# Selective scan, C rows: by DMA through DRAM instead of by matmul and copy; three PSUM pairs in turn

## The reference, cut to what matters

```python
def selective_scan(xs, dts, As, Bs, Cs, Ds, dt_bias):
    delta = jax.nn.softplus(dts + dt_bias[None, :, :, None])
    ...
    def step(h, inp):
        d_t, x_t, B_t, C_t = inp
        dA = jnp.exp(d_t[..., None] * As)
        h = dA * h + (d_t * x_t)[..., None] * B_t[:, :, None, :]
        y = jnp.einsum('bkdn,bkn->bkd', h, C_t)
        return (h, y)
    ...
    return ys + Ds[None, :, :, None] * xs
```

## Time and profile before

| | |
|---|---|
| runs, median (lowest to highest) | 884.73 us (884.34 to 886.65), 3 runs |
| the profiled execution's own time | 886.18 us |
| its span, first to last instruction | 884.3 us |
| mean granted TensorE clock | 0.919 |
| PE, DVE, ACT, POOL busy | 79, 72, 53, 48% of the span |

### The profile page before, as it was taken

How to read it: one execution, slowest core, us unless ns; L and a number is a source line. 1 busy time by engine, 2 the same in 40 slices (tenths; PEclk the granted TensorE clock), 3 DMA queues, 4 the chain that set the end, 5 groups by cost and what they waited for, 6 DMA issues and landing times. The chain is left out here.

```text
span 884.3 us, 7771 instructions
## 1 busy us (share of the span) xinstructions
PE 696.2 (79%) x2716; PEld 366.0 (41%) x2716; DVE 636.9 (72%) x603; ACT 465.5 (53%) x505; POOL 425.5 (48%) x231
## 2 busy tenths in 40 slices
PE   3778788988787878877877786566476769999998
PEld 2443232323222323322322222245324568888886
DVE  5286998998998989998999987945693253334332
ACT  3477578787694787776866734214102223233231
POOL 5035978989989889798797630000051000000000
PEclk9969998999998999999999998879596579999999
DMA  5000000000000000000000006020630000000000
GB/s 154 0 1 1 0 1 1 0 1 0 0 1 0 1 0 1 0 0 1 0 1 0 1 8 254 0 103 1 238 142 1 0 1 1 0 0 0 0 0 24
DMA packets 8287, 20.74 MB, mean 23 GB/s; under 512 B 1333, under 2 KB 2071, under 8 KB 7519
## 3 DMA queue, kind: packets, MB, share of 16 engines
q1 hardware_dynamic: 8256, 20.37, 6.4%
HBM read 19.76 MB, written 0.61 MB: 23 GB/s over the span
## 5 line engine op out<-in xcount | busy, mean ns | idle before, releaser
L552 POOL TENSOR_TENSOR area<-area 128x1024 f32<-128x1024 f32 x127 | 300.1, 2379 | 94.4 <-DVE area L1075 72.7
L1075 DVE TENSOR_TENSOR_SCAN area<-area,ps 128x1024 f32<-128x1024 f32 x128 | 292.6, 2286 | 11.6
L1364 PE MATMUL ps<-area,cst 128*128 128x512 f32 x512 | 263.9, 640 | 30.4 <-POOL area L552 30.2
L735 ACT ACTIVATE area<-ps 128x1024 f32<-128x1024 f32 x127 | 129.8, 1022 | 108.9 <-PE ps L1329 107.8
L1068 DVE TENSOR_TENSOR ps<-ps,area 128x1024 f32<-128x1024 f32 x128 | 154.8, 1210 | 25.9 <-PE ps L1329 25.9
L728 ACT ACTIVATE area<-area,floors,par_sb 128x1024 f32<-128x1024 f32 x128 | 157.4, 1231 | 3.1 <-DVE area L1086 3.0
L1364 PEld LDWEIGHTS ps<-area,cst 128*128 128x128 f32 x512 | 91.1, 196 | 143.9 <-issue 95.8
L1629 PE MATMUL ps<-stack 128*128 128x512 f32 (+3 forms) x768 | 127.8, 326 | 0.4 <-DVE stack L1255 0.4
L1329 PE MATMUL ps<-stack,sel 32*128 32x512 f32 x512 | 86.2, 501 | 48.1 <-DVE area L1075 27.0
L1629 PEld LDWEIGHTS ps<-stack 128*128 128x128 f32 x768 | 117.0, 192 | 11.9 <-issue 2.6
L1329 PEld LDWEIGHTS ps<-stack,sel 32*128 32x128 f32 x512 | 34.8, 186 | 161.9 <-DVE area L1075 61.9
(11 more groups left out here) (285 smaller groups left out, 684.9 us busy)
## 6 DMA issues: line engine op xcount, KB each, us to landing
area<-phi_scaled SPq DMA_DIRECT2D x1, 4104.0 KB, 24.0
area<-in_m_phi_dram SPq DMA_DIRECT2D x4, 1024.0 KB, 8.5
area<-phi_scaled SPq DMA_DIRECT2D x1, 4096.0 KB, 13.7
area<-in_q_t_dram SPq DMA_DIRECT2D x1, 1024.0 KB, 15.2
area<-in_dft_dram SPq DMA_DIRECT2D x1, 784.0 KB
area<-in_m_u_dram SPq DMA_DIRECT2D x1, 768.0 KB, 6.1
area<-in_conv_w_dram SPq DMA_DIRECT2D x1, 576.0 KB, 6.4
cst<-in_consts_dram SPq DMA_DIRECT2D x1, 516.5 KB, 7.0
```

The lines of the kernel that those rows point to most:

```text
L552: pool.tensor_tensor(scan_order(prod[:, u % PRODS, :], k), lines(state[:, u % STATES, :], k), lines(c_sb[:, u % COPIES, :], k), MUL).then_ ...
L735: act.activation(c_sb[:, u % COPIES, :], banks(4), ACT.Copy).then_inc(sig("c_copied"), 1)
L1075: dve.tensor_tensor_scan(state[:, u % STATES, :], decay[:, u % DECAYS, :], drive_pair(u), 0.0, MUL, ADD).then_inc(sig("scanned"), 1)
L1364: mm = pe.matmul(ps[:, 6 + h, :], con("center"), half(prod[:, u % PRODS, :], h), start=False, stop=(u % (UNITS // 2) == UNITS // 2 - 1), s ...
```

## The change

PE no longer spreads C and ACT no longer copies it. When ACT has rounded a block's rows, SP writes the 16 C rows of the two halves from SBUF to a DRAM tensor (two DMAs a block), and for each unit reads one row back, broadcast to 128 partitions, into one of the three C buffers, once the product that used the buffer is made. POOL waits for that DMA instead of the copy.

PSUM pairs 0, 2 and 4 now turn among B spreads and jobs, in the order of a list `slots`; the use of slot s waits until slot s-3 is free, which for a B spread is its scan and for a job ACT's copy. ACT serves a job three units before the unit that it is listed with. PE sums with a lag: at a slot that waited for scan v it sums up to unit v-2, at most two. POOL's preparing sums stand behind units 4, 6, 8 and 10 of a block, one after the other unit; some spectral steps move to later blocks. DVE's list is in the same order as before (drive, scan, unit by unit), with the last C taken from SBUF.

```diff
+        LAG = 2
...
+        c_dram = nc.dram_tensor("c_rows", [BLOCKS, NS, L], F32)
...
+        def c_landed(engine, u):
+            engine.wait_ge(sig(f"c_in_{u % COPIES}"), 16 * (u // COPIES + 1))
...
+        EXTRA = {1: ("spec", 0), 2: ("spec", 1), 3: ("skip", 0), 5: ("var", 0)}
+        JOB_BEFORE = {2: ("gate", 0)}
+        for _n in range(BLOCKS - 1):
+            JOB_BEFORE[NS * _n + 5] = ("z", _n + 1)
+            JOB_BEFORE[NS * _n + 9] = ("rows", _n + 1)
+            if _n in EXTRA:
+                JOB_BEFORE[NS * _n + 13] = EXTRA[_n]
+        slots = []
+        for _u in range(UNITS):
+            if _u in JOB_BEFORE:
+                slots.append(JOB_BEFORE[_u])
+            slots.append(("b", _u))
+        BANK = {turn: 2 * (at % 3) for at, turn in enumerate(slots)}
+        BANK["z", 0], BANK["rows", 0], BANK["gate", 1] = 4, 2, 6
+        FREED = {"z": "relu_ready", "b": "scanned", "rows": "rows_rounded", "gate": "z_ready", "spec": "spec_out",
+                 "skip": "skip_copied", "var": "var_logged"}
+        SERVED = {u - 3: turn for u, turn in JOB_BEFORE.items() if u > 2}
+        OUT_AT, VAR_AT = BANK["b", UNITS - 3], BANK["b", UNITS - 2]
...
         def drive_pair(u):
-            return banks((0, 2)[u % 2])
-
-        Z_AT, ROWS_AT = 1, 2
-        JOBS = {}
-        for _n in range(1, BLOCKS):
-            JOBS[8 * (_n - 1) + Z_AT] = ("z", _n)
-            JOBS[8 * (_n - 1) + ROWS_AT] = ("rows", _n)
-        JOBS[8 + 4], JOBS[8 + 6], JOBS[2 * 8 + 4], JOBS[4 * 8 + 4] = ("spec", 0), ("spec", 1), ("skip", 0), ("var", 0)
-
-        turns = [("z", 0), ("c", 0), ("c", 1)]
-        for _m in range(PAIRS):
-            if _m in JOBS:
-                turns.append(JOBS[_m])
-            turns += [("c", _u) for _u in (2 * _m + 2, 2 * _m + 3) if _u < UNITS]
-            if _m == 0:
...
+            def c_rows_out(n):
+
+                sp.wait_ge(sig("rows_rounded"), n + 1)
+                src = c_raw(n)
+                for h in range(2):
+                    at = 64 + 32 * h
+                    sp.dma_start(c_dram.ap()[n, :, h * HALF:(h + 1) * HALF],
+                                 src[at:at + NS, :]).then_inc(sig("c_rows_out"), 16)
+
+            c_rows_out(0)
+            for u in range(UNITS):
+                n, i = divmod(u, NS)
+                if i == 0:
+                    sp.wait_ge(sig("c_rows_out"), 32 * (n + 1))
+                wait(sp, sig("weighed"), u - COPIES + 1)
+                sp.dma_start(c_sb[:, u % COPIES, :],
+                             c_dram.ap()[n, i:i + 1, :].broadcast_to([P, L])).then_inc(sig(f"c_in_{u % COPIES}"), 16)
+                if i == 10 and n < BLOCKS - 1:
+                    c_rows_out(n + 1)
...
             def weigh(u):
 
                 pool.wait_ge(sig("scanned"), u + 1)
-                pool.wait_ge(sig("c_copied"), u + 1)
+                c_landed(pool, u)
...
+            for u in range(UNITS - 1):
+                n, i = divmod(u, NS)
+                weigh(u)
+                if n < BLOCKS - 1:
+                    if i in (4, 6, 8, 10):
+                        soft_sum(n + 1, (i - 4) // 2)
+                    elif i == 9:
+                        split_rows(n + 1)
...
                 act.wait_ge(sig("rows_done"), n + 1)
                 wait(act, sig("rows_ready"), n)
                 if n:
-                    act.activation(rows_raw, ps[:, 4, :], ACT.Copy)
-                act.activation(high(rows_high), ps[:, (4 if n else 2), :], ACT.Copy).then_inc(sig("rows_rounded"), 1)
+                    wait(act, sig("c_rows_out"), 32 * n)
+                src = ps[:, BANK["rows", n], :]
+                if n:
+                    act.activation(rows_raw, src, ACT.Copy)
+                else:
+                    act.activation(c_raw(0)[64:128], src[64:128], ACT.Copy)
+                act.activation(high(rows_high[0:64]), src[0:64], ACT.Copy).then_inc(sig("rows_rounded"), 1)
...
-            def copy_c(u):
-
-                act.wait_ge(sig("c_spread"), u + 1)
-                wait(act, sig("weighed"), u - COPIES + 1)
-                act.activation(c_sb[:, u % COPIES, :], banks(4), ACT.Copy).then_inc(sig("c_copied"), 1)
...
+            act.preload_act_table_set("silu_and_others")
+            conv_out(1)
+            gate_out(0)
+            gate_out(1)
+            act.preload_act_table_set("natural_log_exp_and_others")
+            act.wait_ge(sig("phi_out"), 16)
+            for u in range(UNITS):
+                n, i = divmod(u, NS)
+                if u + DECAYS < UNITS:
+                    make_decay(u + DECAYS)
+                if u in SERVED:
+                    serve(*SERVED[u])
+                if i == 3 and n < BLOCKS - 1:
                     soft(n + 1, "exp")
                     soft(n + 1, "one_plus")
-                elif p == ROWS_AT and n < BLOCKS - 1:
+                elif i == 4 and n < BLOCKS - 1:
                     soft(n + 1, "log")
                     soft(n + 1, "rest")
...
-            for m in range(PAIRS):
-                n, p = divmod(m, 8)
-                for u in (2 * m, 2 * m + 1):
-                    drive_unit(u)
-                    scan_unit(u)
+            for u in range(UNITS):
+                drive_unit(u)
+                scan_unit(u)
...
+            def slot_free(at):
+
+                kind, i = slots[at - 3]
+                pe.wait_ge(sig(FREED[kind]), i + 1)
 
             def spread_b(u):
+
                 n, b, k, i = block_of(u)
                 if i == 0:
                     pe.wait_ge(sig("rows_ready"), n + 1)
-                wait(pe, sig("scanned"), u - 1)
-                spread(u, 0, (0, 2)[u % 2]).then_inc(sig("b_spread"), 1)
-
-            def spread_c(u):
-                n, b, k, i = block_of(u)
-                if i == 0:
-                    pe.wait_ge(sig("rows_ready"), n + 1)
-                shared_free("c", u)
-                spread(u, 1, 4).then_inc(sig("c_spread"), 1)
+                for h in range(2):
+                    at = 32 * h
+                    mm = pe.matmul(ps[:, BANK["b", u] + h, :], sel[at:at + 32, i, :], b_rows[at:at + 32, n % 2, :],
+                                   start=True, stop=True)
+                mm.then_inc(sig("b_spread"), 1)
...
             pe.wait_ge(*after("sel_ready"))
             spread_b(0)
             spread_b(1)
-            spread_c(0)
             convolution(1, 1)
-            spread_c(1)
+            gate(0)
             pe.wait_ge(sig("consts_in"), 16)
-            for m in range(PAIRS):
-                before, beside = sums_of(m)
-                pe.wait_ge(sig("scanned"), 2 * m + 1)
-                if 2 * m + 2 < UNITS:
-                    spread_b(2 * m + 2)
-                if m in JOBS:
-                    job(*JOBS[m])
-                if m == PAIRS - 1:
-                    pe.wait_ge(sig("first_gated"), 1)
-                    for h in range(2):
-                        project_out(0, h, y_first)
-                for u in before:
-                    sum_state(u)
-                pe.wait_ge(sig("scanned"), 2 * m + 2)
-                if 2 * m + 3 < UNITS:
-                    spread_b(2 * m + 3)
-                if 2 * m + 2 < UNITS:
-                    spread_c(2 * m + 2)
-                for u in beside[:1]:
-                    sum_state(u)
-                if 2 * m + 3 < UNITS:
-                    spread_c(2 * m + 3)
-                for u in beside[1:]:
-                    sum_state(u)
-                if m == 0:
-                    gate(0)
+            scanned, done = -1, 0
+            for at in range(3, len(slots)):
+                kind, i = slots[at]
+                if (kind, i) == ("b", 4):
                     gate(1)
-            sum_state(UNITS - 1)
+                slot_free(at)
+                if kind == "b":
+                    spread_b(i)
+                else:
+                    job(kind, i)
+                if slots[at - 3][0] == "b":
+                    scanned = slots[at - 3][1]
+                if i >= 4 or kind != "b":
+                    for u in range(done, min(done + 2, scanned - LAG + 1)):
+                        sum_state(u)
+                        done = u + 1
+            pe.wait_ge(sig("scanned"), UNITS - 1)
+            pe.wait_ge(sig("first_gated"), 1)
+            for h in range(2):
+                project_out(0, h, y_first)
+            for u in range(done, UNITS):
+                sum_state(u)
```

More of the change, by code:

```diff
@@ L166, in program, with c_raw @@
         high = lambda t: t.bitcast(F32R)
+        def c_raw(n):
+            return rows_raw if n else y_first[:, 0:HALF]
         w_dt_sb = c_sb[0:RANK, 0, :].rearrange("p (a k m) -> p a k m", a=2, k=ND)
@@ L749, in _ @@
             rows_round(0)
-            make_decay(0)
-            make_decay(1)
-            copy_c(0)
-            make_decay(2)
-            make_decay(3)
-            copy_c(1)
+            for u in range(DECAYS):
+                make_decay(u)
             def gate_out(b):
```

(28 more changed lines are left out.)

141 lines of the change are left out of this document (42 added, 99 removed).

## The result

The kernel after takes 863.95 us median (863.09 to 865.1, 4 runs), the kernel before, measured beside it, 885.39 us (884.34 to 886.65, 4 runs): ratio 0.9758, 95% interval 0.9739 to 0.9777, faster. The forecast was 866, range 861 to 877. The profiled execution took 863.64 us, its span 861.9.

The account below looks back on a forecast made before the run. DVE was taken to bound the scan stage, with holes ended by spreads on PE. The terms -25.9 + 1.5 + 3.6 + 2.3 = -18.5 us gave 867.7 from the profiled 886.18, by the median 866; range 861 to 877.

Parts of the forecast that it names:

- What bounds: Scan stage: DVE bounds it, with holes that each end with a spread on PE; drives wait 25.9 us.
- -25.9 for the waits: Scan stage: all 25.9 us that DVE's drives wait for spreads on PE go.
- The third pair as the cause: PSUM in the scan stage: B spread waits for scan u-3 instead of u-2, 7.0 us before its drive.
- The start, +1.5: B spread of unit 5, behind z, skip product and sum: 1.5 us late, between 0 (full clock) and 5.1 (lower clock).
- C by DMA, 3.5 us, cost 0: Each unit's C row broadcast to 128 partitions in 3.5 us, within the 8.1 us before its weighing: cost 0.
- the ring: C buffers: weigh, load, weigh over three units, period (load + 2.38) / 3, if the load takes over 8.1 us.
- POOL's backlog: Units 4 to 10 of a block: POOL falls behind by up to 5.3 us, 9.3 allowed: cost 0.
- PE clock 1.00: Scan stage: PE idles 1.0 us in every 3.5 and keeps clock 1.00 through the stage.
- The end, +3.6 + 2.3 = +5.9: After the last scan: two more units of sums left, +3.6 us; some 4.6 us at half clock lose 2.3.
- A: Projections in the stage: PE loses the clock, 1.4 us late at eight of 18 jobs, 11 us, 877; chance 0.12.
- B: C load takes over 8.1 us; at 9 us the period is 3.79, +37, so 903; chance 0.08.
- C: ACT serves a projection late, the spread inheriting its pair waits; 15.7 of 25.9 us stay, 882; chance 0.06.

Follow-up runs that it names:

- run 3: Kernel after, but B spreads alternate between two PSUM pairs and all jobs have the third, C still by DMA: 864.27 us, ratio 0.976 to the kernel before.
- run 4: Kernel after, but C spread by PE and copied by ACT again, no DMA, three pairs turning among B, C and jobs: 917.5 us, ratio 1.0358 to before.
- run 7: Kernel after with two C buffers instead of three: 864.5 us, ratio 0.9747 to the kernel before; with one buffer: 1188 us, one run.
- run 5: Kernel after with two pairs for B, one for jobs, and sums up to unit 124 drained before the last projection: 863.93 us, ratio 0.9722 to before.
- Run 6: Kernel after with PE's sums one unit behind instead of two: 867.11 us, ratio 0.9767 to the kernel before.
- Run 2: Kernel after with the sums of units 123 and 124 placed before the wait for the last projection: 859.61 us, ratio 0.9702 to the kernel before.
- run 1: The kernel after measured once more, unchanged: 864.77 us, ratio 0.9771 to the kernel before.

## Why the prediction was right, step by step

- **What bounds.** Right. DVE's holes, all ended by B spreads, were the whole price, and the earlier trace rows had it in one number.
- **-25.9 for the waits.** Right in kind, 1.7 short. From the first drive to the end of the last scan 27.6 us went. Most of the rest is overlap. Two rows in order of time, after:

```profile
52.36 2.29 DVE L1088 TENSOR_TENSOR_SCAN area<-area,ps 128x1024 f32<-128x1024 f32 x1
...
54.57 1.21 DVE L1081 TENSOR_TENSOR ps<-ps,area 128x1024 f32<-128x1024 f32 x1
```

  An unhindered drive starts 0.08 us before the scan ahead has ended (54.65), while a wait is counted from the scan's end; and a drive after a wait takes 1.23 instead of 1.21 us. With 13 waits that is 1.3 us.
- **The third pair as the cause.** Half wrong. The prediction put the gain down to two things at once, C gone from PE and ACT and B spreads a unit earlier. Runs 3 and 4 part them: C by DMA with two pairs gives 0.976, three pairs without the DMA 1.0358 (in the one order that was tried). The earlier spread gave 0.9 us of slack at the change of image, and no time that the runs could tell.
- **The start, +1.5.** The mechanism was right and the size a toss: 0 in the first execution, 1.51 and 1.53 in two others with the same order there, by whether z gets the full clock after 1.42 us of idleness. The ends 0 and 5.1 were rightly kept.
- **C by DMA, 3.5 us, cost 0.** 3.7 measured, and POOL never waited for it in either execution of the kernel after. The clean price of the ring is in run 7. That 128 partitions read the same 4 KB did no harm: 512 KB took 3.7 us, the median of 128 loads in a row.
- **POOL's backlog.** At most 5.3 us was predicted. Scan 61, and the weighing of units 61 and 62, after:

```profile
258.89 2.29 DVE L1088 TENSOR_TENSOR_SCAN area<-area,ps 128x1024 f32<-128x1024 f32 x1
```

```profile
265.53 4.66 POOL L576 TENSOR_TENSOR area<-area 128x1024 f32<-128x1024 f32 x2
```

  265.53 less 261.18, the end of the scan, is 4.35 us, the largest before the end of the stage. In the first block it is 3.3 us: there the four preparing sums take 2.4 us each, not the 2.95 I charged; the mean of the third of them over the blocks is 2.9. Cost 0, as predicted.
- **PE clock 1.00.** Right in every stretch from 60 to 480 us. The reason given, short idleness, is not the whole of it: in run 5 the clock fell at 282 us behind a hole of 0.44 us. Run 6 shows how near the edge is.
- **The end, +3.6 + 2.3 = +5.9.** Measured +5.6: 3.9 for the sums and 1.7 for the clock, which only the projection paid. Run 2 takes both back.
- **Not foreseen.** The first drive at 44.0 instead of 45.5, and +1.1 behind the last sum. The sum on paper was -18.5, the execution gave -22.5: the start term that did not come (1.5), the first drive (1.5), the overlap (1.7), 0.3 at the end, less 1.1. By the medians the change gave 21.4 us where 18.5 were forecast. So 866 against 863.95 is a sum with the main term right and several small ones missed, nearly all to the same side, not precision.
- **Rivals.** A: in the kernel after PE lost its clock at no projection between the start and the end of the stage; it lost it at z of the start in run 1, and at the output projection, both of which the forecast had in its own terms. B: its ring is real, its threshold far off. C: no wait came back behind ACT; run 4 shows what it looks like when it does.

Left open: why the first drive comes 1.0 to 2.2 us earlier in all eleven profiles of changed kernels; 0.75 us of it is there already at the end of DVE's first wait for PE, at 7.54 us before and 6.79 after, and no run was made on it. And why 359.2 to 362.5 us follow the last sum (369.4 with one buffer): 359.2 to 360.3 in four executions (before, after twice, two buffers), 361.9 to 362.5 in the other seven, the drained sums among them. From 60 to 100 us behind the last sum the granted clock was 0.88 in the four and 0.81 to 0.84 in the seven; whether the clock leads or follows was not tried.

## What to carry to other kernels

When a result goes from one engine through another before the first can go on (PE, ACT, PE), look at what stands behind it in order: the price is not the copy but the critical work queued behind it. A row that all partitions need can be broadcast by DMA with latency hidden by buffers; count the ring, (load + use) / buffers, against the period; here two buffers (3.0 us against 3.50) were enough and the third changed nothing. When a step lags, count what is left for the end of the loop: drain it in a hole that is there anyway, which here also kept TensorE's clock up for what followed.

## What the runs showed of the hardware

- The granted clock after 1.42 us of idleness is not settled: z at about 54.8 us took 1.98 us in three executions (after, the drained sums, two buffers) and 3.78 in two (after once more, the drained sums once more), with the same instructions ahead. With up to 1.1 us of idleness in every 3.5 it stayed at 1.00 for 420 us in the kernel after. Yet at the change of image, with two pairs and 0.44 to 0.45 us of idleness, the skip product took 1.98 us in run 3 and 3.64 in run 5. After 4.6 the projection took 3.45 to 3.67 us in four executions of four. An estimate that hangs on it needs both ends.
- DVE, ACT and POOL kept their durations beside a DMA stream of 150 GB/s into the same SBUF: scan 2286 ns, drive 1206 ns (1210 before), decay 1239 ns (1231 before), weighing 2373 ns (2379 before).
- A broadcast of one 4 KB row to 128 partitions lands in 3.5 us with nothing else queued and in 3.7 in the stream.
